# Experts of a fused RWKV + MoE layer: groups of 1, 2, 2, 2, 1 batch elements instead of four groups of 2, and a new step table

## What is computed

```python
# block 1: RWKV time mixing and channel mixing
xa = ln(x); xs = shift(xa)
k, v = mix(xa, xs, tm_k) @ Wk, mix(xa, xs, tm_v) @ Wv
r = sigmoid(mix(xa, xs, tm_r) @ Wr)
x = x + (r * wkv(w, time_first, k, v)) @ Wo          # wkv: scan over the tokens
xc = ln(x); xs = shift(xc)
x = x + sigmoid(mix(xc, xs, cm_r) @ Wcr) * (square(relu(mix(xc, xs, cm_k) @ Wck)) @ Wcv)

# block 2: attention with 16 heads of width 8, then a mixture of 8 experts, 2 per token
h = layernorm(x)
x = x + softmax(q k^T / sqrt(8)) v @ Wo
m = layernorm(x)
probs = softmax(m @ Wg); wts, idx = top_k(probs, 2); wts = wts / sum(wts)
x = x + sum_k wts_k * (gelu(m @ W1[idx_k] + b1[idx_k]) @ W2[idx_k] + b2[idx_k])
```

## Time and profile before

| | us |
|---|---|
| median of 3 runs | 1064.16 (1063.0 to 1066.33) |
| the profiled execution | 1063.83, its span 1061.8 |
| PE busy in the span | 830.0 (78%) |
| DVE, ACT, POOL busy | 658.8, 589.1, 422.5 |
| mean granted TensorE clock | 0.862 of full speed |
| DMA moved | 109.59 MB |

### The profile page before, as it was taken

The page is one execution under the profiler, slowest core; times in us unless marked ns, Lnnn a source line. Parts: engine busy times, 40 slices in busy tenths (PEclk is TensorE's granted clock), DMA queues, the critical chain, the costliest instruction groups (busy, mean ns, idle before and its releaser), DMA issues. The chain is left out here.

```text
span 1061.8 us, 15480 instructions
## 1 busy us (share of the span) xinstructions
PE 830.0 (78%) x5245; PEld 512.3 (48%) x5245; DVE 658.8 (62%) x1331; ACT 589.1 (55%) x984; POOL 422.5 (40%) x545
## 2 busy tenths in 40 slices
PE   2166888778877888999998899889988898747760
PEld 1143445344434445555556455655554555546760
DVE  3528757875787677867876798589665673211101
ACT  1123455535643568768766877687667777423330
POOL 4454215325522543264327336843260370035005
PEclk9576797768766889999989999899899999977885
DMA  6400231990000042232213223405132352538742
GB/s 194 126 10 1 90 99 46 292 288 30 1 1 1 30 149 83 84 112 84 82 58 103 90 83 108 137 16 160 58 102 80 100 156 78 166 127 266 228 151 59
DMA packets 99164, 109.59 MB, mean 103 GB/s; under 512 B 7647, under 2 KB 83086, under 8 KB 99086
## 3 DMA queue, kind: packets, MB, share of 16 engines
q1 hardware_dynamic: 94990, 100.20, 30.1%
q0 software_dynamic: 4096, 8.40, 2.4%
HBM read 72.63 MB, written 35.93 MB: 102 GB/s over the span
## 5 line engine op out<-in xcount | busy, mean ns | idle before, releaser
L1380 DVE TENSOR_REDUCE QA<-psB 128x2 f32<-128x1024 f32 x256 | 312.0, 1219 | 153.1 <-PE psB L1076 152.2
L894 ACT ACTIVATE PT<-psB 128x1024 f32<-128x1024 f32 x256 | 261.8, 1023 | 146.3 <-PE psB L1092 145.5
L1076 PE MATMUL psB<-KT,Q 24*128 24x512 f32 x512 | 140.4, 543 | 31.4 <-DVE QA L1380 30.8
L1092 PE MATMUL psB<-Q,KT 32*128 32x512 f32 x512 | 136.4, 529 | 30.7 <-ACT PT L894 24.2
L1104 PE MATMUL psV<-PT,VA 128*32 128x512 f32 x1024 | 157.3, 690 | 0.4
L1169 PE MATMUL psA<-MX,WB 128*128 128x128 f32 x736 | 107.9, 305 | 22.7 <-ACT H L922 17.3
L922 ACT ACTIVATE H<-psA,WB 128x128 f32<-128x128 f32 x368 | 102.3, 377 | 28.4 <-PE psA L1169 27.9
L1092 PEld LDWEIGHTS psB<-Q,KT 32*128 32x128 f32 x512 | 50.4, 193 | 133.8 <-ACT PT L894 79.5
L1169 PEld LDWEIGHTS psA<-MX,WB 128*128 128x128 f32 x736 | 100.3, 217 | 30.0 <-issue 16.5
L1179 PE MATMUL psY<-WB,H 128*128 128x128 f32 x736 | 99.1, 282 | 0.7 <-ACT H L922 0.7
L1179 PEld LDWEIGHTS psY<-WB,H 128*128 128x128 f32 x736 | 89.2, 193 | 19.4 <-issue 14.0
(11 more groups left out here) (195 smaller groups left out, 1340.7 us busy)
## 6 DMA issues: line engine op xcount, KB each, us to landing
WB<-w_rows SPq DMA_DIRECT2D x92, 578.0 KB, 5.0
pairs<-XT SPq DMA_DIRECT2D x2, 4608.0 KB, 16.9
outs<-XT SPq DMA_DIRECT2D x2, 4608.0 KB, 30.1
XT<-pairs SPq DMA_DIRECT2D x92, 64.0 KB
outs<-YT SPq DMA_DIRECT2D x92, 64.0 KB
w_rows<-WB SPq DMA_DIRECT2D x8, 578.0 KB, 3.1
X<-in_L_attn_x_dram SPq DMA_DIRECT2D x8, 256.0 KB, 2.9
H<-in_L_ffn_W_dram SPq DMA_DIRECT2D x8, 256.0 KB, 4.2
```

Of the source, the lines that this page charges most:

```text
L894: act.activation(PT[:, (c % 2) * G + j:(c % 2) * G + j + 2, :], psT, ACT.Exp, scale=SCALE).then_inc(t_taken.sem, 1)
L1076: pe.matmul(psS[:, h, :], chunk(Q1[r, g, :], c), KT[r, g, :], start=True, stop=True).then_inc(s_full.sem, 1)
L1092: pe.matmul(psT[:, h, :], chunk(KT[r, g, :], c), Q2[r, g % 2, :], start=True, stop=True).then_inc(t_full.sem, 1)
L1380: dve.tensor_reduce(QA[:, c, g * G + j:g * G + j + 2, RM], psS, AX_X, ALU.max).then_inc(s_taken.sem, 1)
```

## The change

The groups become [0], [1,2], [3,4], [5,6], [7], with 15, 23, 23, 23, 15 tiles and 5, 8, 8, 8, 5 windows (34 in all, 99 tiles instead of 92). A window may start at any slot: the list START gives 56, 64, ..., 88 for group 0, 120 to 176 for group 1, 184 to 240 for group 2, 248 to 283 in steps of 5 for group 3 and 288 to 320 in steps of 8 for group 4. BEGIN and END_OF hold each group's first start and last start + 8, and the steps at a group's beginning and end are counted from these. On SP pass_on is taken apart: the rows of window w+2 are loaded first, when PE's and ACT's use of the rows of window w is over (u.taken), then come, after y_taken of window w, the weights of w+2 and then the stores of w. Waits are added where the two DRAM areas are used again (a group's first scatter waits for the stores of the group before the last, a group's first store for the gathers of the group before the last). The area grows from 72 to 80 blocks of 128 rows. Most entries of the tables move, the farthest by five and a half slots.

```diff
-    GROUPS = B // 2
-    TILES = 4 * T // TW + E - 1
...
-    WINDOWS = -(-TILES // WIN)
...
+    MEMBERS = [[0]] + [[b, b + 1] for b in range(1, B - 1, 2)] + [[B - 1]]
+    GROUPS = len(MEMBERS)
+    GROUP_OF = {b: group for group in range(GROUPS) for b in MEMBERS[group]}
+    TILES = [2 * len(m) * T // TW + E - 1 for m in MEMBERS]
...
+    WINDOWS = [-(-tiles // WIN) for tiles in TILES]
...
-        FIRST_WINDOW = 11
+        AHEAD = 3
+        STRIDE = [8, 8, 8, 5, 8]
+        START, BEGIN, END_OF = [], [], []
+        for group in range(GROUPS):
+            BEGIN.append(max([SLOTS * (MEMBERS[group][-1] + 1) + PER * AHEAD] + [at + STRIDE[group - 1] for at in START[-1:]]))
+            START += [BEGIN[-1] + STRIDE[group] * w for w in range(WINDOWS[group])]
+            END_OF.append(START[-1] + PER)
...
+            def rows_in(w):
...
+                if w >= 2:
+                    u = use(members(w - 2)[0], "x")
+                    sp.wait_ge(u.taken, u.after)
+                for n in members(w):
+                    i = within(n)
+                    both = sp.value_load(TMAP[i:i + 1, group % 2:group % 2 + 1], min_val=0, max_val=E * (BLOCKS - 1) - 1)
+                    blocks[n], experts[n] = both >> 3, both & (E - 1)
+                    sp.dma_start(XT[:, w % 2, i % WIN, :], XS[group % 2].rearrange("(b p) n -> b p n", p=P)[blocks[n]]).then_inc(xt_in[w % 2], 16)
+
+            def weights_in(w):
...
                 if w >= 2:
                     sp.wait_ge(y_taken.sem, y_taken.at(w - 2, 1))
                 for n in members(w):
...
+                    sp.dma_start(WB[:, ring(n), :], WS[experts[n]]).then_inc(w_in[ring(n)], 16)
...
-            TILE = {7: (tile_step(0, pass_on),)}
-            GROUP = {82: (begin(0),), 94: (begin(1),), 179: (keep(0),), 181: (keep(1),)}
+            TILE = {9: (tile_step(0, next_rows),), 11: (tile_step(0, next_weights), tile_step(0, rows_out),)}
+            GROUP = {-2: (begin(0),), 3: (begin(1),)}
+            END = {20: (keep(0),), 49: (keep(1),)}
```

```diff
-            POST = {3.5: (c_norm,), 15: (positions,), 16.5: (scatter(0),), 25: (scatter(2),)}
+            POST = {7: (c_norm,), 15.5: (positions,), 19: (scatter(0),), 24.5: (scatter(2),)}
...
-            POST = {5.5: (c_ctx,), 6: (c_out,), 10.5: (c_norm,), 11: (c_logits,), 13.5: (rank,)}
+            POST = {6: (c_ctx,), 7: (c_out,), 14: (c_norm,), 16.5: (c_logits,), 18.5: (rank,)}
```

214 lines of the change are left out of this document (118 added, 96 removed), and 4 rows, old and new, of the table USES.

## The result

| | before | after |
|---|---|---|
| median, same chip (range) | 1065.01 (1063.0 to 1066.33) | 1008.02 (1001.99 to 1008.7) |
| ratio, 95% interval | | 0.945 (0.942 to 0.947) |
| the profiled execution, its span | 1063.83, 1061.8 | 1008.64, 1006.9 |
| mean granted clock | 0.862 | 0.902 |
| end of the last context piece (CX) | 914.3 | 895.0 |

The kernel is 57 us faster, at the edge of the range forecast: 0.945 of 1064.16 is 1005.4, a little under the low end of 1007. But the sum was wrong in two places that partly cancel: the attention ended 26 us earlier than forecast, and the part behind it was 10 us longer. That the time comes so near the range is therefore luck: with the part behind the attention as forecast it would have been about 998.

A forecast was written before the change was run, and what follows sets the result against it. PE was taken as fullest in the turns, with engines waiting in line behind the attention. Attention end 921.3, plus 24.0, 21.5, 37.2, 3.7 and 15.8, gave a span of 1023.5, hence 1026 us; range 1007 to 1043.

The forecast's parts named there:

- Step 1: Attention turns: extra windows cost nothing before slot 248 and 5.0 us in turn 7; +5, bounds -3 and +14.
- Step 2: Steps changing places within turns: only POOL's scatters ahead of the head's norm cost; +2 us, bounds -14 and +15.
- the moves pay: Rival, attention turns: new places fill PE's idle gaps, winning 2 us in each of seven turns; 1010 us, chance 0.15.
- Step 3: End of context to the router's positions: 21.0 us before, +3 for added PE work, bounds 0 and +8.
- Step 4: Router's positions to transposes of group 4's first window: PE's former wait filled with work; 21.5 us, bounds 21 and 25.
- Step 5: Last group: five windows instead of eight, each after the first 7.2 us; 37.2 us, bounds 36 and 46.
- My three margins: Last group: SP's work, the weights' loop and bytes each checked against 7.2 us a window; none binds, all near.
- the loads still set the pace: Rival, last group: loads hold windows to 9 us or more; 1036 to 1042 us, chance 0.13.
- Step 6: Kernel's end: last output to first gather 3.7 us, then 15.8 with eight gathers fewer, bounds 14.4 and 17.
- 0.95 or more: Sign, from the router's positions to the last output: PE's granted clock at this level.
- DVE's wait for rsH: Sign, ahead of the head's ZA: a wait, none before, of 0.4 to 1.5 us in turns 1 to 5.
- The rival of the scatters ahead of rsA: Late router puts scatters and positions ahead of rsA; DVE stands 7.1 us in each of seven turns; 1076 us, chance 0.03.

The follow-up runs named there:

- e13: The changed kernel again, unchanged, beside the kernel before and each half of the change: 1005.5 us, ratio 0.943.
- e15: The kernel before with only the changed kernel's step tables (new places; old groups, windows and SP steps): 1029.6 us, ratio 0.966.
- e16: The changed kernel with the old step tables (old places; new groups, windows and SP steps): 1055.4 us, ratio 0.986.
- e11: The changed kernel with one POOL step back, norm_2 at 25.5 behind all eight scatters instead of 21.5: 1062.6 us in a slower set.
- e8: The changed kernel with combine(0) five slots later, a group's first two windows loading weights before rows, and begin(1) four slots later: 1001.7 us, ratio 0.940.
- e4: The changed kernel with four groups of two elements again, windows every 8 slots: 1048.4 us, ratio 0.927, in a slower set.
- e14: The kernel before, unchanged, run again for its profile: 1064.5 us, ratio 0.998.
- e7: The changed kernel with the fourth pair of projections' transposes and their ACT copies about three slots later, near their old places: 1021.9 us, ratio 0.961.
- e6: The changed kernel with POOL's four step tables of the kernel before: 1049.75 us, ratio 0.985.
- e17: The kernel before with the router's steps at or near their new places on all engines and POOL's norm_2 between the scatters: 1076.1 us, ratio 1.008.
- e12: The kernel before with only POOL's norm_2 moved, to 20, between the fourth and fifth scatter: 1115.9 us against 1130.3, ratio 0.987.
- e18: The changed kernel with only DVE's combine(0) five slots later, at 18 for 13: 1009.7 us, ratio 0.946.
- e9: The kernel before with only the changed kernel's step tables, in a slower set: 1061.1 us, ratio 0.938.
- e10: The changed kernel with the step tables of the kernel before, in a slower set: 1109.8 us, ratio 0.981.

## Why the prediction was wrong, step by step

**Step 1, the windows in the turns (+5): near in size, but split the other way.** I had nothing in the seven turns and 5.0 in the eighth; in e13 against e15 they cost 5.8 in the seven and 1 in the eighth. Three profiles of the changed kernel have 688.0, 693.0 and 694.7 for the seven turns, and the latter two 66 for the eighth, so this is 6 to 13 and 1 to 3; with those two, of other sets, the sum is at or over my bound of 14. My reading that a turn is no longer for its windows holds where the clock was low: the second turn takes 95.9 us at 0.86 without windows (e15) and 95.6 at 0.95 with two (e13). At the old places the windows cost 20.4, outside my bound.

**Step 2, the moves within the turns (+2, bounds -14 and +15): the term that failed.** In the seven turns it is -38 by e15, and -53 if measured with the windows in place (e16 against e13); the eighth turn takes 3.1 of the first back. Three errors. I priced one move, POOL's, by the wait that it adds ahead of the head's norm, from rows of the kernel before, and took rsA to come 0.9 earlier; the wait for rsA in fact grew from 1.3 to 2.2 us a turn. The price depends on the other moves: with them in place undoing it costs some 27 us (e11). I put all others at nothing, with a bound of 2 us a turn from the length of single waits, though most entries of the tables move (POOL's tail_shift by six and a half slots, more than the five and a half that I named). And I counted waits alone: the moves took away 12 us of waiting, and the same matmuls took 26 less at a clock of 0.94 in place of 0.90. The rival "the moves pay" named the gaps but not the clock, at 2 us a turn, with a chance of 0.15; it was 5.5 a turn. That its 1010 lies near the 1008 measured is luck: it had the rest of the sum as forecast.

**Step 3, CX to POS (24.0): right**; 895.0 to 918.2 is 23.2.

**Step 4, POS to transposes (21.5): right**; 918.21 to 940.12 is 21.9.

**Step 5, the last group (37.2, bounds 36 and 46): the second term that failed**, 48.7, 11.5 too low. The first window took 12.5 for my 8.4: its weights were issued 2.9 us behind its rows, themselves waiting for the scatters, and not 1. e8 shows that the order of the two only trades one wait for another. The other four took 36.2 for my 28.8, of which 7.0 is the gap of 14.2. My three margins (SP, the weights' loop, the bytes) were not the whole list: outputs are 7.2 apart in e4 and in three of four gaps of e8, where DVE is free, and what broke the rhythm was DVE waiting in a combine for gathers, which waited for POOL, and POOL for a store that SP had behind begin(1). I had named the gathers of elements 5 and 6 as covered by the last group, without asking what DVE holds back while it waits for them. The rival "the loads still set the pace" has the right size, 9 us a window, by luck: the largest gap is DVE's. Behind the first window, waits for weights are there only in the last two (1.55, and 1.4 that the view gives to "issue"), after DVE's late output had put off their issue (967.57).

**Step 6, the end (3.7 + 15.8): right within 1.5**, 3.8 and 14.3, the second at its lower bound.

The clock behind the attention: 1.00, 0.90 and 0.95 to the last output, where I asked for 0.95 or more. In the turns, where the clock mattered most, it was 0.90 in e14 and 0.94 in e15. The rule of the Trainium skill, TensorE: Matmul & The Clock Gate, section HAM oscillation, was weighed only for the last group; what it says of waits for DMA and slow bursts goes the same way as the pair e14 and e15, but e7 and e11 show that the sum of the idle time does not tell the clock. DVE's wait for rsH was there as forecast, but in 2 turns of six, 2.3 us in all (e13). The rival of the scatters ahead of rsA was held off by the split; e6 and e11 show it as waits of 5 to 6 us a turn.

**What stays open.** Which moves bring the 38 us. The router alone costs 9 in the seven turns (e17), undoing the fourth transposes costs 12 (e7), undoing norm_2 some 27 (e11), and norm_2 alone brings 14 us of the whole time in a slower set (e12). They don't add up; the places work as a set. What raised the clock in the turns is open too, and so is how the 29 to 37 us behind the attention divide among groups of one, steps of 5 and SP's order, since no set at 1065 us has them apart. Why the kernel before takes 1130 us in some sets isn't settled either, since it has no profile from them. Loading weights first was not tried alone, and none of the variants beats the changed kernel by more than the measurement can tell.

## What to carry to other kernels

Where one engine is the bound and its clock is not at full speed, a reordering can pay twice: by the waits that it removes, and by the busy time of that engine at another clock. Here the second was twice the first, and the idle time alone did not foretell it. A move's price read from the kernel before holds only beside the other steps of the kernel before; when a whole table changes, bound the sum of the moves by all the idle time and the clock that is missing, not by single waits. And for every step that waits for a transfer late in a chain, ask what else stands behind it in its engine's queue: a combine ahead of an output tile opened a gap of 7 us here. Then ask it again of the next queue: moving the combine alone (e18) moved the gap and gained nothing, because a store behind the combine held SP's loads.

## What the runs showed of the hardware

The same program took 1130 us in two sets and 1065 in three, 6% apart, each within 1% over its 7 to 13 runs. The record gives the same chip number, 5, for set 1 (1130) and set 2 (1065), so the chip alone may not be the reason. Two orderings differ in how much they lose in the slower sets: the new places' seven turns are 682 and 688 us, the old ones' with the windows 741 and 758. In the slower sets the waits carry a releaser, "remote", that no profile of the other sets has on DVE, and longer ones of "issue" on PE. PE in e9 (behind the attention), and DVE's sums in e10 (230 to 830 us):

```profile
958.05 3.55 PE L1169 MATMUL psA<-MX,WB 128*128 128x128 f32 x16 [10.33 <-issue]
```

```profile
DVE QA L1421 <- remote: 17.7, 4, 7.5
```

What is behind these names the runs do not tell.
